# A recurrent scan of 128 steps: state and input stacked in one 128-row tile, one state and one output matmul a step, its input loaded from the loop's last iteration

## The chip, the core and the metric

The kernel runs on one core of a Trainium2 chip. The metric is the device time of one execution in microseconds (us). A core has TensorE (matmuls, fp32 here, in two passes each), VectorE, ScalarE, GpSimd and SyncE (SP), which issues the DMAs. Each works through its own instruction stream; they meet at semaphores.

## The reference, cut to what matters

The program is four attention blocks over 128 sequences of 128 positions and 256 features, and then a small recurrent layer, the scan. The change touches the scan:

```python
U = (xn @ W_in.T + b_in) @ Bmat            # 128 sequences x 128 positions x 64

def step(s, u_t):
    s = silu(s @ A.T) + u_t                # 64 states a sequence
    return (s, s)
_, states = lax.scan(step, zeros((128, 64)), U.transpose(1, 0, 2))
ssm_out = einsum('tbs,sh->bth', states, Cmat)   # 64 -> 256
x = residual + ssm_out
return x + mod[:, None, :]
```

All is fp32. The sequence of steps can't be parallelised: step n needs the state of step n-1, of all 128 sequences.

## The kernel before

There are four parts. A **prologue** loads weights (SP, lines 372 to 410) and prepares constants. The **loop** works on two sequences an iteration, in software pipelining: `drive` (line 235) issues, on each engine, a list of steps with a lag each; after the last full iteration come six partial ones, in which ever fewer steps are left. It leaves two tensors in HBM: `residual` (x before the scan, with mod added) and `u_turned` (U with the 64 states outermost, for each sequence 64 rows of 128 positions). SP's last steps in the loop are the stores of both. A **small block** (lines 1368 to 1384) clears tiles and loads the scan's constants and U. The **scan** (from line 1386) is the last block.

In the scan of before, half the sequences are on partitions 0 to 63 and half on 64 to 127. `u_all` (in the tile scan_u) holds U, `a2` is A.T twice on the diagonal of a 128x128 tile, and gbuf holds g = silu(...) of a step, without U, in four buffers of 64 columns. In step n:
- TensorE adds A u(n-1) (line 1460) and A g(n-1) (line 1463) in one bank, with 64 columns each;
- ScalarE applies silu to it into gbuf (line 1479);
- GpSimd adds g and u in two instructions of 64 partitions into the tile `sblk`, one for each half of the sequences (line 1437), since the output needs the sequences beside each other;
- TensorE makes the output of step n-1, with sblk as the stationary operand and C of 64 rows used twice as the moving one (line 1450, 256 columns), in one of two banks;
- VectorE adds it to the residual in SBUF (line 1488).

The elements of u_all that one step reads are 128 positions, 512 bytes, apart. The residual comes in 16 chunks of 8 positions, 1 MB each, in four buffers (SP: `load`, line 1402, and `store`, line 1406). On the four engines the first 32 steps are written out and the other 96 are a loop of three turns of 32 steps (`chunks`), with addresses and semaphore values from registers there.

Of the kernel before, what the change touches and what calls it, by code (L numbers as in the profile page):

```python
# [19 lines left out]
ALU = mybir.AluOpType  # L20
# [4 lines left out]
G = 2  # L25
NG = B // G
# [208 lines left out]
def drive(eng, rings, handlers, engine):  # L235
# [15 lines left out]
    for i in range(max(NG, LAGS + 1), NG + LAGS):  # L251
        body(i, LAGS + 2 + i - NG, False)


def build(nc, dram):
# [6 lines left out]
    with ExitStack() as ctx:  # L262
# [3 lines left out]
        def sem(name):  # L266
# [10 lines left out]
        wt = {n: sb("w_" + n, [128, DH, D]) for n in  # L277
              ("q1", "k1", "v1", "q2", "k2", "v2", "fc1", "fc2", "q3", "k3", "v3", "o3")}
# [13 lines left out]
               ("X", "XR", "CB", "Z1", "X1", "X1r", "Z2", "X2", "X3", "CC", "HC", "NF", "CR", "NC", "X4", "X5",  # L292
                "H5", "ATT", "X6", "H6")}
        trn_all = sb("turned", [128, 19, DH, W])
# [3 lines left out]
        scan_u = sb("scan_u", [128, B // 2 * S])  # L298
        keys12 = scan_u[:, 0:4 * DH * W].rearrange("p (k a h w) -> p k a h w", k=2, a=DH, h=2)
        keys1, keys2 = keys12[:, 0, :, :, :], keys12[:, 1, :, :, :]  # L300
        keys3 = sb("keys3", [128, DH, W])
        half_of = sb("half_of", [128, 2])
        vp1 = sb("vp1", [128, G, L0_HEADS, 32])
        vp2 = sb("vp2", [128, G, L0_HEADS, 32])
        vp3 = sb("vp3", [128, G, L3_HEADS, 64])
        vn1 = sb("vn1", [128, G, D])
        vn2 = sb("vn2", [128, G, D])
# [52 lines left out]
        ctxb_sb = scan_u[:, 0:S // 2 * NP].rearrange("p (s n) -> p s n", n=NP)  # L360
# [9 lines left out]
        with nc.Block() as block:  # L370
            @block.sync
            def _(sp):
                n = 0
                for name, t in wt.items():
# [38 lines left out]
        with nc.Block() as block:  # L413

            @block.vector
            def _(dve):
# [3 lines left out]
                nc.vector.memset(ones_b[:], 1.0)  # L420
                nc.vector.memset(half[:], -0.5)
# [75 lines left out]

        with nc.Block() as block:
            @block.sync
            def _(sp):  # L500
# [29 lines left out]

                def store_u(g):
# [4 lines left out]
                drive(sp, [], dict(self_in=dict(load=load_self), self_att=dict(load=load_again), ctx_in=dict(load=load_ctx),  # L536
                                   pair=dict(load=load_pair), mix_out=dict(load=load_mod, store=store, store_u=store_u)), "sp")
                for w in latest(res_out.done(NG - 1), u_out.done(NG - 1)):
                    sp.wait_ge(*w)

# [718 lines left out]
            def _(pool):  # L1259
# [74 lines left out]
                def mod_(g):  # L1334
# [13 lines left out]

        HB = B // 2
        NB = 4
        CHUNKS = S // TC
        u_all = scan_u[:].rearrange("p (b t) -> p b t", t=S)
        a2 = nat["X"][:, 0, 0:128]
        c2 = nat["CB"][:, 0, :]
        gbuf = [nat["Z1"][:, n // 2, (n % 2) * HB:(n % 2) * HB + HB] for n in range(4)]
        sblk = [nat["Z2"][:, n, 0:128] for n in range(2)]
        res_t = [trn_all[:, 4 * n:4 * n + 4, :, :].rearrange("p k a w -> p (k a w)").rearrange("p (t d) -> p t d", d=D)
                 for n in range(NB)]  # L1360
        vbank, obank = pbank[0:2], pbank[2:4]

        started, scan_in, v_ready, g_ready, s_ready, o_ready, out_ready = (
            sem(n) for n in ("started", "scan_in", "v_ready", "g_ready", "s_ready", "o_ready", "out_ready"))
        res_in = [sem(f"res_in{n}") for n in range(NB)]
        chunk_out = [sem(f"chunk_out{n}") for n in range(NB)]

        with nc.Block() as block:
            @block.vector
            def _(dve):  # L1370
                nc.vector.memset(nat["X"][:], 0.0)
                nc.vector.memset(nat["Z1"][:], 0.0)
                nc.vector.memset(nat["Z2"][:], 0.0).then_inc(started, 1)
                dve.wait_ge(started, 1)

            @block.sync
# [182 lines left out]
```

## Time and profile before

| | us |
|---|---|
| median of 3 runs | 4868.46 (4865.99 to 4876.72) |
| profiled execution | 4871.74, its span 4869.9 |
| loop with its ends, to the last store of u | up to 4678.9 |
| small block, until the scan opens | 4708.23 |
| scan | 4708.2 to 4869.9 |

The page gives TensorE 95% busy over the span, VectorE 76%, ScalarE 57%, GpSimd 45%. These shares are those of the loop. The mean granted TensorE clock is 0.975 of full; it is 0.5 while TensorE idles between loop and scan. In a timeline row the first two numbers are start and duration in us; what stands in brackets is the idle time of the engine before it and who ended it. PEld is the load of the stationary operand, PE the passes of the moving one; "x2" merges the two passes of an fp32 matmul. SPq is the issue of a DMA.

### The profile page before, as it was taken

Reading aid. Unit: us, or ns where it says so; the run is one execution under the profiler, and the core shown is the slowest. Engines: PE = TensorE matmul, PEld = TensorE weight load, DVE = VectorE, ACT = ScalarE, POOL = GpSimd, SP = SyncE. Lnnn points to the kernel's source line nnn. Section 1 sums busy time; section 2 is a strip of 40 time slices with the busy share of each in tenths; the row PEclk is TensorE's granted clock in tenths of the full one; section 3 lists DMA queues with packets and bytes.
Section 4 is the critical chain, followed back from the end, with each engine's and each line's share of the span. In section 5 each row is a group of like instructions: output and inputs, shape, how many; then the busy total and the mean of one; then the engine's idle time right before and its main releaser. Section 6 shows DMA issues by size and latency. Waiting matters only on the chain. (4 is left out here: it accounts for less than half of the span.)

```text
span 4869.9 us, 129469 instructions
## 1 busy us (share of the span) xinstructions
PE 4604.4 (95%) x38435; PEld 3800.8 (78%) x38563; DVE 3718.0 (76%) x10020; ACT 2760.2 (57%) x5761; POOL 2179.1 (45%) x2308
## 2 busy tenths in 40 slices
PE   2899999999999999999999999999999999999858
PEld 1678888888888888888888888888888888887647
DVE  2677888788878887887788888878888888788623
ACT  0456665666566656655665666556656665666411
POOL 0344444444444445444544454444444444444325
PEclk9899999999999999999999999999999999999879
DMA  3000000000000000000000000000000000000045
GB/s 92 18 19 22 26 22 28 21 24 25 28 21 22 26 28 21 21 27 28 21 21 27 28 21 21 27 28 21 21 27 28 21 21 27 27 21 20 20 122 199
DMA packets 139569, 156.21 MB, mean 32 GB/s; under 512 B 23942, under 2 KB 126667, under 8 KB 134859
## 3 DMA queue, kind: packets, MB, share of 16 engines
q1 hardware_dynamic: 139210, 152.93, 10.2%
q14 instruction: 316, 2.58, 0.2%
q8 instruction: 43, 0.70, 0.1%
HBM read 115.01 MB, written 37.88 MB: 31 GB/s over the span
## 5 line engine op out<-in xcount | busy, mean ns | idle before, releaser
L868 ACT ACTIVATE probT<-bank 128x512 f32<-128x512 f32 x1280 | 713.0, 594 | 604.9 <-PE bank L612 597.1
L1002 DVE TENSOR_REDUCE mx<-bank 128x4 f32<-128x512 f32 x1280 | 848.6, 680 | 200.2 <-PE bank L593 131.9
L1013 DVE TENSOR_TENSOR prob<-bank,mx 128x512 f32<-128x512 f32 x1280 | 870.9, 685 | 158.4 <-PE bank L612 137.4
L858 ACT ACTIVATE prob<-prob 128x512 f32<-128x512 f32 x1280 | 785.1, 629 | 189.1 <-DVE prob L1013 188.2
L848 ACT ACTIVATE turned<-bank 128x512 f32<-128x512 f32 x960 | 561.2, 601 | 438.2 <-PE bank L548 331.2
L1266 POOL TENSOR_TENSOR rs_ln<-ve_ln,half 128x2 f32<-128x2 f32 x320 | 226.1, 706 | 1182.5 <-DVE ve_ln L981 1182.5
L612 PE MATMUL bank<-ident,prob 128*128 128x128 f32 x5120 | 700.1, 278 | 43.1 <-ACT outT L878 41.3
L612 PEld LDWEIGHTS bank<-ident,prob 128*128 128x128 f32 x5120 | 587.6, 145 | 111.0 <-ACT prob L858 61.5
L597 PE MATMUL bank<-scan_u,turned 32*128 32x256 f32 x4096 | 493.7, 404 | 4.0 <-DVE X L1186 3.0
L1313 POOL TENSOR_SCALAR scan_u<-turned,half_of 128x512 f32<-128x512 f32 x256 | 399.4, 1571 | 118.7 <-ACT turned L848 118.7
L597 PEld LDWEIGHTS bank<-scan_u,turned 32*128 32x128 f32 x4096 | 321.1, 186 | 163.1 <-issue 142.4
L1275 POOL TENSOR_TENSOR X<-X,row_ln_g 128x512 f32<-128x512 f32 x192 | 244.3, 1273 | 446.9 <-DVE X L990 446.9
L556 PE MATMUL bank<-turned,w_q 128*128 128x256 f32 x1536 | 373.0, 386 | 1.4 <-ACT turned L848 1.4
L556 PE MATMUL bank<-turned,w_k 128*128 128x256 f32 x1536 | 372.1, 385 | 0.0
L564 PE MATMUL bank<-w_v,turned 128*128 128x256 f32 x1536 | 359.1, 383 | 0.5 <-ACT probT L868 0.3
L564 PEld LDWEIGHTS bank<-w_v,turned 128*128 128x128 f32 x1536 | 287.5, 190 | 41.3 <-ACT probT L868 0.4
L556 PEld LDWEIGHTS bank<-turned,w_k 128*128 128x128 f32 x1536 | 283.8, 191 | 39.0 <-issue 1.3
L556 PEld LDWEIGHTS bank<-turned,w_q 128*128 128x128 f32 x1536 | 279.9, 192 | 33.0 <-ACT turned L848 2.2
L642 PE MATMUL bank<-probT,vp 128*32 128x128 f32 x8192 | 293.2, 278 | 1.6 <-DVE vp L1100 1.0
L878 ACT ACTIVATE outT<-bank 128x512 f32<-128x512 f32 x384 | 221.7, 595 | 112.4 <-PE bank L642 90.5
L642 PEld LDWEIGHTS bank<-probT,vp 128*32 128x32 f32 x8192 | 201.8, 110 | 91.4 <-issue 64.8
L655 PE MATMUL bank<-ident,outT 128*128 128x128 f32 x1536 | 248.5, 286 | 3.2 <-ACT outT L878 3.2
(210 smaller groups left out, 8886.5 us busy)
## 6 DMA issues: line engine op xcount, KB each, us to landing
X<-in_x SPq DMA_DIRECT2D x64, 256.0 KB, 2.8
XR<-in_x SPq DMA_DIRECT2D x64, 256.0 KB, 2.7
CB<-in_ctx SPq DMA_DIRECT2D x64, 256.0 KB, 2.9
CC<-in_ctx SPq DMA_DIRECT2D x64, 256.0 KB, 2.7
mod<-mod_rows SPq DMA_DIRECT2D x64, 256.0 KB, 3.8
residual<-X SPq DMA_DIRECT2D x64, 256.0 KB, 2.2
turned<-residual SPq DMA_DIRECT2D x16, 1024.0 KB, 6.8
out<-turned SPq DMA_DIRECT2D x16, 1024.0 KB, 4.8
```

The lines of the kernel that those rows point to most:

```text
L556: last = nc.tensor.matmul(t[:, m * W:(m + 1) * W], w[:, a, m * 128:(m + 1) * 128], src[:, a, :], start=(a == 0), stop=(a == DH - 1))
L564: last = nc.tensor.matmul(t[:, b * D:(b + 1) * D], src[:, a, b * S:(b + 1) * S], w[:, a, :], start=(a == 0), stop=(a == DH - 1))
L597: last = nc.tensor.matmul(t[:, a * W:(a + 1) * W], QT[p][rows_, a, b * S:(b + 1) * S], KEYS[p][rows_, a, :, b * S:(b + 1) * S], start=(p ! ...
L612: last = nc.tensor.transpose(t[:, h * 128:(h + 1) * 128], src[:, h, :], ident[:])
L642: last = nc.tensor.matmul(t[k * 32:(k + 1) * 32, r * 128:(r + 1) * 128], VP[p][:, b, 4 * r + k, :], src[:, k, :], start=True, stop=True)
L655: last = nc.tensor.transpose(t[:, c * 128:(c + 1) * 128], outsT.of(key)[:, c, :], ident[:])
L848: nc.scalar.activation(dst, banks.of(f"{unit}.{name}")[:, 0:n], ACT.Copy).then_inc(*st["act"].mark(name))
L858: nc.scalar.activation(flat(t), flat(t), ACT.Exp, scale=SCALE[p]).then_inc(*st["act"].mark(f"exp.{b}{r}"))
L868: nc.scalar.activation(flat(t), banks.of(f"{att}.turn.{b}{r}")[:, :], ACT.Copy).then_inc(*st["act"].mark(f"probT.{b}{r}"))
L1002: nc.vector.tensor_reduce(m[:], banks.of(f"{att}.tile.{b}{r}")[:, :].rearrange("p (h t) -> p h t", h=4), AX, ALU.max)\
L1013: nc.vector.tensor_tensor(t[:], banks.of(f"{att}.tile.{b}{r}")[:, :].rearrange("p (h t) -> p h t", h=4), maxes.of(f"{att}.max.{b}{r}")[:]. ...
L1313: last = nc.gpsimd.tensor_scalar(KEYS[p][:, :, c, :], KT[p][:], half_of[:, c:c + 1], None, ALU.mult)
```

## The change

**One tile.** `shared`, 128 partitions x 16384, takes what scan_u held, and during the loop also eight weight tiles, the two x tiles and others. In the scan its partitions 64 to 127 hold U for all 128 sequences (`fresh`), and partitions 0 to 63 hold g of all steps (`state`), which ScalarE writes. So column t of sequence b has g above and u below. `a_two` is A.T twice, one below the other (columns 64 to 127 are zero), `c_two` is C twice. One matmul with 128 rows then sums both parts: A g + A u for the state, C g + C u for the output. There is no sum on GpSimd, and the output has four banks. TensorE's 128 steps are written out now; ScalarE, VectorE and SP keep their loops.

**The load.** `drive` takes a function `meanwhile` that is called at the start of the last partial iteration, only on SP: `scan_early` waits for the last readers of what it overwrites and loads U and four residual chunks of 126 sequences. The last two sequences' part comes behind the loop. The small block is gone; a_t and c_mat are loaded at the start of the prologue.

```diff
-def drive(eng, rings, handlers, engine):
+def drive(eng, rings, handlers, engine, meanwhile=None):
     for i in range(max(NG, LAGS + 1), NG + LAGS):
+        if meanwhile is not None and i == NG + LAGS - 1:
+            meanwhile()
         body(i, LAGS + 2 + i - NG, False)
...
+        shared = sb("shared", [128, B * S])
+        wt = {n: lent(DH, D) for n in ("q1", "k1", "v1", "q2", "k2", "v2", "fc1", "fc2")}
+        x_own, x_again, vn1, vn2 = (lent(G, D) for _ in range(4))
+        a_two = sb("a_two", [128, 128])
+        c_two = sb("c_two", [128, D])
-        scan_u = sb("scan_u", [128, B // 2 * S])
...
+                for k in range(2):
+                    r = slice(NS * k, NS * k + NS)
+                    sp.dma_start(a_two[r, 0:NS], dram["a_t"]).then_inc(loaded, 16)
+                    sp.dma_start(c_two[r, :], dram["c_mat"]).then_inc(loaded, 16)
...
+        EARLY = B - G
+        gu = shared[:].rearrange("p (b t) -> p b t", t=S)
+        state, fresh = gu[0:NS, :, :], gu[NS:2 * NS, :, :]
+        vbank, obank = pbank[0:2], pbank[2:6]
+        def scan_input(sp, b):
+            sp.dma_start(fresh[:, b, :], u_d[b].rearrange("b n s -> n b s")).then_inc(u_in, 16)
+            for k in range(NB):
+                sp.dma_start(res_t[k][b, :, :], res_d[b, k * TC:(k + 1) * TC, :]).then_inc(res_in[k], 16)
...
+                def scan_early():
+                    n = NG - 1
+                    for w in latest(self_in["pe"].done("xT", n), ..., u_out.done(n - 1), res_out.done(n - 1)):
+                        sp.wait_ge(*w)
+                    scan_input(sp, slice(0, EARLY))
...
                 for w in latest(res_out.done(NG - 1), u_out.done(NG - 1)):
                     sp.wait_ge(*w)
+                scan_input(sp, slice(EARLY, B))
...
-        with nc.Block() as block:     # memsets; loads of a_t, c_mat and u, 64 partitions each
...
-            @block.gpsimd             # s = g + u, two tensor_tensor a step
...
-                    nc.tensor.matmul(obank[k][:, 0:D], sblk[k], c2, start=True, stop=True).then_inc(o_ready, 1)
-                        nc.tensor.matmul(v[:, 0:HB], a2, u_all[:, :, bass.ds(n - 1, 1)], start=True, stop=False)
-                        nc.tensor.matmul(v[:, 0:HB], a2, gbuf[(t - 1) % 4], start=False, stop=True).then_inc(v_ready, 1)
+                def output(n):
+                    if n >= 4:
+                        pe.wait_ge(out_ready, n - 3)
+                    nc.tensor.matmul(obank[n % 4][:, 0:D], gu[:, :, n], c_two[:], start=True, stop=True).then_inc(o_ready, 1)
+                pe.wait_ge(u_in, 32)
+                pe.wait_ge(zeroed, 1)
+                for n in range(1, S):
+                    if n >= 2:
+                        pe.wait_ge(g_ready, n - 1)
+                    nc.tensor.matmul(vbank[n % 2][:, 0:B], a_two[:], gu[:, :, n - 1], start=True, stop=True).then_inc(v_ready, 1)
+                    output(n - 1)
...
-                        nc.scalar.activation(gbuf[t % 4], vbank[t % 2][:, 0:HB], ACT.Silu).then_inc(g_ready, 1)
+                        nc.scalar.activation(state[:, :, bass.ds(n, 1)], vbank[t % 2][0:NS, 0:B].unsqueeze(2), ACT.Silu).then_inc(g_ready, 1)
...
+                nc.vector.memset(state[:, :, 0:1], 0.0).then_inc(zeroed, 1)
```

The order of SP's instructions at the end of the loop, before the change (residual and u_turned are the tensors in HBM, started is the semaphore of the memsets):

```order
L529 DMA residual<-X 128x2x256 [waits mix_out_pool_6]
L534 DMA u_turned<-us 64x2x128 [waits mix_out_dve_6]
L498 UNCONDITIONAL_BRANCH [waits u_out,res_out]
L1376 UNCONDITIONAL_BRANCH [waits barrier_Pool_Activation_PE_DVE_SP_release]
L1381 DMA X<-in_a_t 64x64 [waits started]
L1382 DMA CB<-in_c_mat 64x256
L1383 DMA scan_u<-u_turned 64x64x128
L1381 DMA X<-in_a_t 64x64
L1382 DMA CB<-in_c_mat 64x256
L1383 DMA scan_u<-u_turned 64x64x128
L1368 UNCONDITIONAL_BRANCH [waits scan_in]
```

And the same place after it:

```order
L567 DMA residual<-X 128x2x256 [waits mix_out_pool_6]
L532 DMA shared<-u_turned 64x126x128 [waits ffn_pe_3,ctx_att_pe_3,pair_pe_4,ctx_att_pe_2,real_pe_4,ctx_in_dve_3,mix_in_pe_4,self_att_pe_1,mix_in_pe_5,self_att_dve_2,u_out,self_in_pool_1,res_out,self_in_dve_2,self_in_pe_0]
L534 DMA turned<-residual 126x2048 x4
L584 DMA u_turned<-us 64x2x128 [waits mix_out_dve_6]
L532 DMA shared<-u_turned 64x2x128 [waits u_out,res_out]
L534 DMA turned<-residual 2x2048 x4
L536 UNCONDITIONAL_BRANCH
```

The last store of residual stays first; the large loads of the scan stand between it and the last store of u_turned.

On ScalarE, the loop of the scan before the change (one step is two rows; v_ready is counted up by the state matmul):

```order
L1478 REGISTER_ALU [waits s_ready]
L1479 ACTIVATE Z1<-bank0 128x64 [waits v_ready]
L1478 REGISTER_ALU [waits s_ready]
L1479 ACTIVATE Z1<-bank1 128x64 [waits v_ready]
L1391 REGISTER_ALU
```

And after it:

```order
L1459 REGISTER_ALU
L1460 ISA [waits v_ready]
L1460 ACTIVATE shared<-bank1 64x128
L1459 REGISTER_ALU
L1460 ISA [waits v_ready]
L1460 ACTIVATE shared<-bank0 64x128
```

The wait for the matmul stood on the ACTIVATE, and stands now on the instruction ahead of it, which works out the destination's address.

## Rows read from the trace of the kernel before

**Rows 1.** Who waited for whom, from 4650 us: total us, times, longest us
```profile
ACT Z L1479 <- PE bank L1463: 125.4, 126, 2.2
DVE turned L1488 <- PE bank L1450: 98.5, 126, 1.1
```

**Rows 2.** Timeline of one step of the scan: start us, duration us, engine
```profile
4783.86 0.30 PEld L1463 LDWEIGHTS bank<-Z,X 128*128 128x128 f32 x2
4783.95 0.35 PE L1463 MATMUL bank<-Z,X 128*128 128x64 f32 x2
...
4784.34 0.22 ACT L1479 ACTIVATE Z<-bank 128x64 f32<-128x64 f32 x1 [0.86 <-PE bank L1463]
...
4784.55 0.70 PE L1450 MATMUL bank<-CB,Z 128*128 128x256 f32 x2 [0.25 <-POOL Z L1437]
4784.78 0.78 POOL L1437 TENSOR_TENSOR Z<-Z,scan_u 64x64 f32<-64x64 f32 x2 [0.29 <-issue]
```

**Rows 3.** Timeline: the first and the last of the scan's 127 ACTIVATEs
```profile
4709.52 0.23 ACT L1479 ACTIVATE Z<-bank 128x64 f32<-128x64 f32 x1
...
4863.15 0.22 ACT L1479 ACTIVATE Z<-bank 128x64 f32<-128x64 f32 x1 [0.77 <-PE bank L1463]
```

**Rows 4.** Lines 1460 and 1450, 4709.6 to 4711.5: ns min/median/max (clock 0.5)
```profile
L1460 PE MATMUL bank<-scan_u,X x2: 314/360/407, 4710.1 to 4710.2; 128*128 128x64 f32 x2
L1450 PE MATMUL bank<-CB,Z x4: 634/688/741, 4709.1 to 4711.4; 128*128 128x256 f32 x4
```

**Rows 5.** Lines 1450, 1463, 1460, 4716 to 4865: ns min/median/max (clock 1.0)
```profile
L1450 PE MATMUL bank<-CB,Z x248: 379/407/483, 4716.1 to 4864.7; 128*128 128x256 f32 x124
L1463 PE MATMUL bank<-Z,X x244: 235/264/275, 4716.8 to 4862.8; 128*128 128x64 f32 x122
L1460 PE MATMUL bank<-scan_u,X x244: 269/287/354, 4716.6 to 4862.7; 128*128 x96, 128*128 128x64 f32 x26
L1460 PEldq FUSED_REGOPS  x96: 37/37/51, 4747.2 to 4862.0; - x96
```

**Rows 6.** VectorE groups in the prologue: shapes, busy us, mean ns, idle
```profile
L447 DVE TENSOR_REDUCE X<-scan_u 128x64 f32<-128x4096 f32 x2 | 14.0, 6978 | 7.5 <-DMA scan_u<-in_ctxb 7.5
...
L428 DVE MEMSET vp<- 128x16 f32 x1 | 0.1, 72 | 0.0
L426 DVE MEMSET y<- 128x10 f32 x1 | 0.1, 67 | 0.0
```

**Rows 7.** Timeline at the loop's end: weights that wait for an ACTIVATE
```profile
4665.31 0.60 ACT L848 ACTIVATE turned<-bank 128x512 f32<-128x512 f32 x1 [2.92 <-PE bank L548]
4665.96 0.50 PEld L564 LDWEIGHTS bank<-w_o,turned 128*128 128x128 f32 x2 [1.15 <-ACT turned L848]
```

**Rows 8.** Timeline of SP's DMA issues between loop and scan
```profile
4675.73 0.38 SPq L529 DMA_DIRECT2D residual<-X  x1
4678.89 0.60 SPq L534 DMA_DIRECT2D u_turned<-us  x1
4683.22 0.54 SPq L1381 DMA_DIRECT2D X<-in_a_t  x1
4683.81 0.59 SPq L1382 DMA_DIRECT2D CB<-in_c_mat  x1
4684.45 0.63 SPq L1383 DMA_DIRECT2D scan_u<-u_turned  x1
4685.12 7.08 SPq L1381 DMA_DIRECT2D X<-in_a_t  x1
...
4692.88 0.62 SPq L1383 DMA_DIRECT2D scan_u<-u_turned  x1
4708.23 1.29 SPq L1402 DMA_DIRECT2D turned<-residual  x3
```

**Rows 9.** A stretch of three residual loads: last column GB/s
```profile
4712.00:4717.00 5.00, 3.35 (x23) 2.95 (x22) 1.78 (x5) 0.67 (x3) 2.35 (x7) 1.00 1.02 431
```

**Rows 10.** DMA issues, 4676 to 4712 us: count, KB each, median us to landing
```profile
u_turned<-us SPq DMA_DIRECT2D x1, 64.0 KB, 2.1
```

More of the change, by code:

```diff
@@ L420, in _ @@
                 nc.vector.memset(ones_b[:], 1.0)
+                nc.vector.memset(a_two[:, NS:128], 0.0)
                 nc.vector.memset(half[:], -0.5)
@@ L536, in _ @@
                 drive(sp, [], dict(self_in=dict(load=load_self), self_att=dict(load=load_again), ctx_in=dict(load=load_ctx),
[L537 removed]
+                                   pair=dict(load=load_pair), mix_out=dict(load=load_mod, store=store, store_u=store_u)), "sp", scan_early)
                 for w in latest(res_out.done(NG - 1), u_out.done(NG - 1)):
                     sp.wait_ge(*w)
+                scan_input(sp, slice(EARLY, B))
             @block.tensor
@@ L1346, in _ @@
                     real=dict(**ln_pow("ln5", "real")), mix_out=dict(**ln_pow("ln6", "mix_out"), mod=mod_)), "pool")
[L1351 to L1366, printed above, removed]
-        with nc.Block() as block:
[L1369 to L1376, printed above, removed]
-            def _(sp):
-                sp.wait_ge(started, 1)
-                for k in range(2):
-                    r = slice(NS * k, NS * k + NS)
-                    sp.dma_start(nat["X"][r, 0, NS * k:NS * k + NS], dram["a_t"]).then_inc(scan_in, 16)
-                    sp.dma_start(nat["CB"][r, 0, :], dram["c_mat"]).then_inc(scan_in, 16)
-                    sp.dma_start(u_all[r, :, :], u_d[k * HB:(k + 1) * HB].rearrange("b n s -> n b s")).then_inc(scan_in, 16)
-                sp.wait_ge(scan_in, 96)
         with nc.Block() as block:
@@ L1422, in _ @@
                     sp.wait_ge(chunk_out[k], 16 * (CHUNKS // NB))
-            @block.gpsimd
-            def _(pool):
-                def body(c, k, _):
-                    for t in range(TC):
-                        n = c * TC + t
-                        waits = []
-                        if at_least(n, 1):
-                            waits.append((g_ready, n))
-                        if at_least(n, 2):
-                            waits.append((o_ready, n - 1))
-                        waits_apart(pool, prep, *waits)
-                        for half_ in range(2):
-                            r = slice(NS * half_, NS * half_ + NS)
-                            last = nc.gpsimd.tensor_tensor(sblk[t % 2][r, half_ * HB:(half_ + 1) * HB], gbuf[t % 4][r, :],
-                                                           u_all[r, :, bass.ds(n, 1)].rearrange("p b t -> p (b t)"), ALU.add)
-                        last.then_inc(s_ready, 1)
-                chunks(pool, body)
@@ L1466, in _ @@
-                chunks(pe, body)
-                output(S - 1, (S - 1) % 2)
+                def output(n):
[9 more added lines that the diff above has]
+                    output(n - 1)
@@ L1469, in _ @@
+                pe.wait_ge(g_ready, S - 1)
+                output(S - 1)
             @block.scalar
```

65 lines of the change are left out of this document (32 added, 33 removed).

## The prediction

> **What bounds the kernel now.** I read the page's slices first: 39 of 40 show the pipelined loop, in which the change moves no instruction, and the last holds the scan over the 128 positions. So only three stretches can move: the prologue, the hand-over between loop and scan, and the scan. Next I read the waits from 4650 us on [rows 1]. In the scan ScalarE stands 125.4 us waiting for the state matmul, VectorE 98.5 us for the output matmul; nothing is busy all the time, so it is a cycle of dependences. One step of its timeline [rows 2] shows which one: the state pass ends (4783.95 + 0.35 = 4784.30), ScalarE starts at 4784.34 and ends at 4784.56, GpSimd starts the sum only at 4784.78, and TensorE starts an output at 4784.55 that had waited for the sum before. From the first ScalarE step (4709.52) to the last (4863.15) [rows 3] are 153.6 us for 126 steps, 1.22 us each. From the last to the end of the span are 6.7 us.
>
> **The step after the change.** GpSimd leaves the cycle, and TensorE issues two matmuls instead of three. The outputs have four banks, so VectorE's addition does not hold them. What is left is one chain: weights of the state matmul, its two passes (fp32 runs as two) of 128 columns, ScalarE, and back. TensorE's own work besides, the output, has two passes of 256 columns; it lies beside ScalarE.
>
> Cost of a column. At the granted clock of 0.5 (1.2 GHz) a pass of 256 columns takes 634 ns and one of 64 takes 314 [rows 4]: 320 ns for 192 columns, 1.67 ns each, so 0.83 ns at the full clock (2.4 GHz). At the full clock 256 columns take at least 379 ns [rows 5], which is 213 + 166 of pipeline. A pass of 64 neighbouring columns (line 1463) should be 53 + 166 = 219, and its shortest is 235. But line 1460, whose 64 columns lie 512 bytes apart in scan_u, takes at least 269: 269 - 166 = 103 ns, 1.61 ns a column, about twice. At the half clock the same line shows nothing of this (314 is from it). The new moving operand is always of this kind, 128 columns 512 bytes apart, so a pass costs 206 ns and not 107. VectorE pays alike: its sum over elements 256 bytes apart takes 6978 ns for 4096, 1.70 ns each [rows 6]. The Trainium skill (SBUF — State Buffer, section Door 1: The DMA port swizzle) says that SBUF has lines of 16 bytes and that each access that goes to a new line pays a penalty; by it the passes are slow as taken here, and without it a step would be two times 99 ns shorter. The trace agrees for reads.
>
> One step, while ScalarE's addresses are constants (steps 1 to 31): load of weights 108 ns (the two loads of line 1463 in rows 2 span 0.30 at 0.19 each, so the second starts about 0.11 behind the first), first pass 206, second pass 206 + 166, to ScalarE 40 (rows 2: 4784.30 to 4784.34), ScalarE 275, back to TensorE 50 (an ACTIVATE ends at 4665.91, the weights that wait for it load at 4665.96) [rows 7]. ScalarE's 275: 64 elements take 0.22 us and 512 take 0.60 [rows 2, 7], 0.85 ns each, so 64 more are 55. Sum 1.05 us. TensorE alone would need 2 x 206 + 2 x 213 = 0.84 us, with the weight loads beside the passes; even if the strided weights of the output load at half speed (206 ns, which the trace does not show) they lie beside passes of at least that length. So the chain decides.
>
> In the 96 steps of the loop there is something more. Today ScalarE's destination is one of four fixed buffers, and the wait for the matmul sits on the ACTIVATE itself. Now the destination is a column whose address comes from a register: the order shows an ISA row (the address calculation, which carries the wait) ahead of each ACTIVATE, so the ACTIVATE is only sent off when the matmul is done. Nearest rows: this calculation takes 37 to 51 ns on TensorE [rows 5], and GpSimd, which today does the same for scan_u, starts 0.22 us after the ScalarE step that it waits for [rows 2], against 0.05 where the wait sits on the instruction [rows 7]. So the price is between 0.04 and 0.17 us; I take 0.12, nearer to GpSimd since it is the same construction. Loop step: 1.17 us.
>
> Scan from first to last ScalarE step: 30 x 1.05 + 96 x 1.17 = 143.8, and 0.7 for some three steps at the half clock, since TensorE comes from idleness: 144.5 against 153.6. **Gain 9.1 us.** Behind the last step GpSimd's sum is gone and the load of strided weights comes, 5.9 against 6.7: **gain 0.8**.
>
> **The hand-over.** Today SP sends the last residual store at 4675.73, the last u at 4678.89, and after a barrier and three memsets the two halves of u at 4684.45 and 4692.88; the last block opens at 4708.23 [rows 8]. The new early load stands in SP's program behind the last residual store, and that waits for GpSimd's last instruction until 4675.7. So it is not sent an iteration earlier, but at 4675.73 + 0.38 and fifteen waits that are long fulfilled, about 4676.9: 7.5 us sooner than today. And it is larger: the input of 126 sequences and four residual chunks (4.1 MB of input, 4.1 MB of residual), and only then the store of the last u, on which the last two sequences' input depends. All are on one queue: in today's order the second a_t load, sent from 4685.1 to 4692.2 behind the first half of u, took 7.1 us to send. Input: today 23.8 us from the first issue to the opened block, of which I put 0.4 down to the barrier (an estimate, from 0.1 to 0.8), so landed at 4700.3. Residual: at 431 GB/s [rows 9] 9.6 us: 4709.9. Last u: 64 KB, 0.3 us; late input: 2.1 us from issue to landing, as the last u today [rows 10], and SP sends four more small loads (0.63 for the first, 1.29 for three of the others: 2.3 us) before it comes to the barrier: 4712.5. With barrier 0.3 the block opens at 4712.8, against 4708.23: **loss 4.5 us**. Today VectorE also waits for its first residual chunk when the scan opens; that stall is in the 153.6 already. Bounds: 3 (the barrier does not wait for the small loads) to 7. If the last u got in between, the start would be at some 4702, a gain of 6; the order of the queue speaks against it. The Trainium skill (DMA: Bandwidth & Descriptors, section Why a DMA increments its semaphore by 16 and not by 1) says that a DMA runs on the largest number of engines up to 16 that divides its slowest dimension; 126 rows would get 14, an estimate of 1.4 us more for the four residual loads, by which the loss would be 5.9. No run here shows it yet.
>
> **The prologue.** Four more loads stand first in SP's program; the same loads took 0.54 and 0.59 us to send today [rows 8], 2.4 with gaps. Part goes where SP stands at a full queue later: between 0 and 2.4, I take **loss 2**. The memset of a_two is 0.1 us, inside that.
>
> **Sum.** -9.1 - 0.8 + 4.5 + 2 = -3.4 us on the profiled execution's 4871.74 (its span is 4869.9). The median of the runs shown is 4868.46, 3.3 lower; I subtract the same amount: 4865.1 us. A change of 0.2% (9.7 us) is about what a measurement of this kernel can tell from none, so this is no change.
>
> **Rivals.** (1) The stride costs nothing (the ends of matmuls are modelled, so 269 might be a model's). Then the step is 0.198 us shorter, 126 x 0.198 = 25 us: 4840. Against it stand two engines that agree, and the half clock, where it vanishes. Chance 0.12. (2) The address calculation is hidden or costs its 0.04: 96 x 0.08 to 0.12, 8 to 11 us: 4856. For it: ScalarE has 0.77 us idle in each step; against it: the wait sits on it, so it cannot run ahead. Chance 0.20. (3) Slower: ScalarE's write pays for the stride too. It writes 128 elements, 512 bytes apart, and at 1.61 instead of 0.83 ns they take 100 ns more on the chain: 126 x 0.1 = 12.6 us, 4878. It turns slower than before as soon as a written element costs 0.21 ns more than today (3.4 us over 126 x 128 elements). Against it: a memset of 16 elements 256 bytes apart takes 72 ns, one of 10 neighbours 67 [rows 6], 0.8 ns for each of six more, so a short strided write pays nothing on VectorE. The skill's rule does not set writes apart, and by it this is the result. Chance 0.16. (4) The change does not load early in effect: the queue makes the start later still (7 us or more, 4868 and above). Chance 0.07. The forecast has the rest, 0.45.
>
> **How the numbers follow.** Forecast and (4) are within 0.2% nearly always; (1) is faster always, (2) about half the time, and in the forecast a smaller calculation with a smaller stride gives faster once in eight: 0.12 + 0.10 + 0.05, about 0.27. Slower needs (3) with little help from the hand-over, or two of the high bounds: 0.18. Same 0.55. The range leaves out most of (1) and takes in (3): 4846 to 4881.
>
> **What would show it.** In the new profile: the ACTIVATE of 128 elements lasts 275 ns (370 or more: rival 3); the state matmul's shortest first pass 206 + 166 = 372 ns (273: rival 1); the ScalarE steps lie 1.05 us apart in the first 31 and 1.17 in the loop (equal: rival 2); the first TensorE instruction of the scan stands between 4714 and 4716, 2 us of it from the prologue. The forecast is wrong if TensorE, or VectorE, is what ScalarE's successors wait for, or if the loop before the scan changes by more than 2 us.

## The result: 0.5% slower

| | before | after |
|---|---|---|
| median, us | 4868.66 (6 runs, 4862.24 to 4876.72) | 4893.49 (6 runs, 4890.14 to 4900.58) |
| span of the profiled execution | 4869.9 | 4894.6 |

The ratio is 1.0051, 95% interval 1.0039 to 1.0064. The forecast was 4865.1, its range ended at 4881. The two spans differ by 24.7 us, and ScalarE's instructions cut them into five stretches:

| stretch, us | before | after | difference | forecast |
|---|---|---|---|---|
| start to the first ScalarE step of all (prologue) | 96.54 | 99.83 | +3.3 | +2 |
| to the last ScalarE step of the loop | 4579.06 | 4582.91 | +3.9 | 0 |
| to the first ScalarE step of the scan (hand-over) | 33.92 | 42.99 | +9.1 | +4.5 |
| to the scan's last ScalarE step | 153.63 | 162.80 | +9.2 | -9.1 |
| to the end | 6.75 | 6.07 | -0.7 | -0.8 |

The other four stretches are 20.9 us, and they are to be explained. Of the second, 3.9 us, the cause is open. Over the twelve profiles of this case whose kernels have the changed kernel's loop it lies between 4575.0 and 4590.7 us, and of the loop of before there is one profile, so the two profiles alone can't tell. But the medians hint at a real part: for the changed kernel and each of the six experiments below that have several runs, the median differs from that of before by 0.7 to 9.9 us more than its other four stretches do (24.8 against 20.9 for the changed kernel). The prediction named a loop that changes by more than 2 us as a sign that it is wrong, and no experiment here tests why the loop would.

### The profile page after: what moved, and what is told of

The parts are those of the page before. It is cut to its first block and busy times, and to the rows that moved or that the text cites. A ratio compares the mean times of both kernels' runs of the same rounds, so it can differ in the third digit from the quotient of the medians.

```text
span 4894.6 us, 128116 instructions
## 1 busy us (share of the span) xinstructions
PE 4629.2 (95%) x38309; PEld 3801.4 (78%) x38309; DVE 3719.5 (76%) x10019; ACT 2777.4 (57%) x5761; POOL 2084.0 (43%) x2052
## 5 line engine op out<-in xcount | busy, mean ns | idle before, releaser
L607 PE MATMUL bank<-turned,shared 128*128 128x256 f32 x2560 | 616.1, 384 | 0.7 <-ACT turned L899 0.7
L607 PEld LDWEIGHTS bank<-turned,shared 128*128 128x128 f32 x2560 | 465.1, 192 | 56.6 <-ACT turned L899 1.3
L648 PE MATMUL bank<-shared,turned 32*128 32x256 f32 x4096 | 495.8, 406 | 4.0 <-DVE X L1237 3.0
L1364 POOL TENSOR_SCALAR shared<-turned,half_of 128x512 f32<-128x512 f32 x256 | 399.1, 1570 | 123.1 <-ACT turned L899 123.1
L648 PEld LDWEIGHTS bank<-shared,turned 32*128 32x128 f32 x4096 | 323.1, 187 | 163.1 <-issue 142.0
L615 PE MATMUL bank<-shared,turned 128*128 128x256 f32 x1536 | 359.8, 384 | 0.6 <-ACT probT L919 0.3
L615 PEld LDWEIGHTS bank<-shared,turned 128*128 128x128 f32 x1536 | 283.4, 191 | 38.4 <-DVE turned L1160 0.5
L693 PE MATMUL bank<-probT,shared 128*32 128x128 f32 x8192 | 292.8, 278 | 1.9 <-DVE shared L1151 1.0
L1332 POOL TENSOR_TENSOR X<-X,row_ln_b 128x512 f32<-128x512 f32 x192 | 243.7, 1269 | 15.1
L644 PE MATMUL bank<-keys,turned 32*128 32x128 f32 x2048 | 221.6, 286 | 3.8 <-DVE prob L1064 3.2
```

What stands on the lines that cost most here:

```text
L607: last = nc.tensor.matmul(t[:, m * W:(m + 1) * W], w[:, a, m * 128:(m + 1) * 128], src[:, a, :], start=(a == 0), stop=(a == DH - 1))
L615: last = nc.tensor.matmul(t[:, b * D:(b + 1) * D], src[:, a, b * S:(b + 1) * S], w[:, a, :], start=(a == 0), stop=(a == DH - 1))
L648: last = nc.tensor.matmul(t[:, a * W:(a + 1) * W], QT[p][rows_, a, b * S:(b + 1) * S], KEYS[p][rows_, a, :, b * S:(b + 1) * S], start=(p ! ...
L693: last = nc.tensor.matmul(t[k * 32:(k + 1) * 32, r * 128:(r + 1) * 128], VP[p][:, b, 4 * r + k, :], src[:, k, :], start=True, stop=True)
L1364: last = nc.gpsimd.tensor_scalar(KEYS[p][:, :, c, :], KT[p][:], half_of[:, c:c + 1], None, ALU.mult)
```

## The profile after

Waits from 4670 us (who waited for whom: total, times, longest), the answer to [rows 1]:

```profile
ACT shared L1460 <- PE bank L1447: 115.1, 126, 1.2
DVE turned L1471 <- PE bank L1440: 111.5, 128, 1.9
PEld bank L1447 <- ACT shared L1460: 51.6, 126, 0.7
...
PEld bank L1447 <- DMA shared<-u_turned: 40.3, 1, 40.3
```

The cycle is the expected one: ScalarE and TensorE wait for each other 126 times, and GpSimd is gone from it. VectorE waits for TensorE, and in the steps nobody waits for VectorE. The first and the last of the scan's ScalarE rows, and one step of the timeline among the first 31 (start, duration, engine; [rows 2, 3]):

```profile
4725.73 0.38 ACT L1460 ACTIVATE shared<-bank 64x128 f32<-64x128 f32 x1
...
4755.78 0.30 PEld L1447 LDWEIGHTS bank<-shared,a_two 128*128 128x128 f32 x2 [0.35 <-ACT shared L1460]
4755.78 0.75 PE L1447 MATMUL bank<-shared,a_two 128*128 128x128 f32 x2
...
4756.07 0.59 PEld L1440 LDWEIGHTS bank<-c_two,shared 128*128 128x128 f32 x2
4756.35 0.62 PE L1440 MATMUL bank<-c_two,shared 128*128 128x256 f32 x2
4756.57 0.38 ACT L1460 ACTIVATE shared<-bank 64x128 f32<-64x128 f32 x1 [0.84 <-PE bank L1447]
4757.00 0.30 PEld L1447 LDWEIGHTS bank<-shared,a_two 128*128 128x128 f32 x2 [0.34 <-ACT shared L1460]
...
4888.53 0.38 ACT L1460 ACTIVATE shared<-bank 64x128 f32 x1 [0.93 <-PE bank L1447]
```

A step lasts 4757.00 - 4755.78 = 1.22 us, and the load of the output's weights (4756.07 to 4756.66) lies beside the state matmul's second pass (to 4756.53). The durations by line, 4730 to 4888 us (ns min/median/max), answer to [rows 5]:

```profile
L1447 PEld LDWEIGHTS bank<-shared,a_two x246: 185/188/191, 4730.1 to 4887.8; 128*128 128x128 f32 x123
L1447 PE MATMUL bank<-shared,a_two x246: 464/468/472, 4730.1 to 4887.9; 128*128 128x128 f32 x123
...
L1460 ACT ACTIVATE shared<-bank x123: 377/378/381, 4729.6 to 4887.2; 64x128 f32 x95, 64x128 f32<-64x128 f32 x28
L1460 ACTq FUSED_REGOPS  x95: 37/37/37, 4763.9 to 4887.1; - x95
...
L1440 PE MATMUL bank<-c_two,shared x245: 376/379/409, 4729.6 to 4887.2; 128*128 128x256 f32 x123
L1440 PEld LDWEIGHTS bank<-c_two,shared x245: 302/359/366, 4730.4 to 4887.9; 128*128 128x128 f32 x123
```

Written as the forecast wrote it, in us:

| part of a step | forecast | measured |
|---|---|---|
| first load of weights | 0.108 | 0.107 |
| first pass, until the second starts | 0.206 | 0.184 |
| second pass | 0.372 | 0.468 |
| to ScalarE | 0.040 | 0.037 |
| ScalarE | 0.275 | 0.378 |
| back to TensorE | 0.050 | 0.050 |
| sum (first 31 steps) | 1.05 | 1.224 |
| address calculation, loop steps | 0.12 | 0.087 |
| loop step | 1.17 | 1.311 |

The hand-over, in the timeline of SP's issues, the answer to [rows 8]:

```profile
4682.87 0.38 SPq L567 DMA_DIRECT2D residual<-X  x1
4683.76 0.64 SPq L532 DMA_DIRECT2D shared<-u_turned  x1
4684.44 20.62 SPq L534 DMA_DIRECT2D turned<-residual  x4
4705.11 0.61 SPq L584 DMA_DIRECT2D u_turned<-us  x1
4721.88 0.63 SPq L532 DMA_DIRECT2D shared<-u_turned  x1
4722.55 1.34 SPq L534 DMA_DIRECT2D turned<-residual  x4
```

The DMA issues of this stretch (count, KB each, median us to landing) and two windows of it (last columns granted clock, DMA share, GB/s; [rows 9, 10]):

```profile
shared<-u_turned SPq DMA_DIRECT2D x1, 4032.0 KB, 25.9
...
u_turned<-us SPq DMA_DIRECT2D x1, 64.0 KB, 16.7
shared<-u_turned SPq DMA_DIRECT2D x1, 64.0 KB, 2.4
```
```profile
4688.00:4703.00 15.00, 0.00 (x0) 0.00 (x0) 0.00 (x0) 0.00 (x0) 0.00 (x0) 0.50 1.25 176
4706.00:4718.00 12.00, 0.00 (x0) 0.00 (x0) 0.00 (x0) 0.00 (x0) 0.00 (x0) 0.50 0.97 306
```

The store of the last u is sent at 4705.11 and lands 16.7 us later, since the residual is ahead of it on the queue. The last two sequences' input leaves only at 4721.88 and lands 2.4 us later, at 4724.23. Behind it SP sends the four small residual loads before it comes to the barrier, and VectorE clears the first state only behind that:

```profile
4724.56 0.17 DVE L1466 MEMSET shared<- 64x128 f32 x1 [38.56 <-PEq L536]
4724.84 0.29 PEld L1447 LDWEIGHTS bank<-shared,a_two 128*128 128x128 f32 x1 [40.25 <-DMA shared<-u_turned]
```

So TensorE starts at 4724.84. Its row names the input, but that had landed 0.6 us earlier: the barrier and the memset are what ends last.

## Experiments: where the step's time goes

Two steps are given for each kernel: one of the first 31 (ScalarE's addresses constant) and one of the loop. The changed kernel has 1.224 and 1.311.

**Neighbouring columns (e1).** The same tile, viewed with the sequences as neighbours:

```diff
+        gt = shared[:].rearrange("p (t b) -> p t b", b=B)
-  output: gu[:, :, n]          state: gu[:, :, n - 1]     silu: state[:, :, bass.ds(n, 1)]
+  output: gt[:, n, :]          state: gt[:, n - 1, :]     silu: gt[0:NS, bass.ds(n, 1), :]
```

> The changed kernel, but in the scan the tile is read and written as (position, sequence): the 128 elements of a step lie beside each other, for ScalarE's write, for the moving operand of the state matmul and for the stationary one of the output. U is loaded as before, so the numbers pair wrong positions and sequences; the amount of work is the same. Theory S (every access 512 bytes apart costs extra on the chain): ACTIVATE 378 -> 275 ns; state passes from 468 and 468 ns to about 380 (the first, which waits for its weights) and 273; loads of the output's weights 359 -> 190; step 1.22 -> 0.85 us in the 31 written-out steps and 1.31 -> 0.94 in the loop, first to last ACTIVATE 162.8 -> 116 us, span about 4848. Rival X (the chain is long because of 128 columns on 64 partitions and of two matmuls with weights to load, wherever they lie): nothing of this falls by more than 20 ns, span about 4894.

The step behaves as theory S says, in each of its parts, and nothing stays as rival X would have it. Measured: 4854.6 us (one run), steps 0.848 and 0.945, 116.8 us from first to last ACTIVATE. One step of its timeline:

```profile
4749.83 0.30 PEld L1448 LDWEIGHTS bank<-shared,a_two 128*128 128x128 f32 x2 [0.33 <-ACT shared L1461]
4749.84 0.49 PE L1448 MATMUL bank<-shared,a_two 128*128 128x128 f32 x2
...
4750.05 0.30 PEld L1441 LDWEIGHTS bank<-c_two,shared 128*128 128x128 f32 x2
...
4750.36 0.27 ACT L1461 ACTIVATE shared<-bank 64x128 f32<-64x128 f32 x1 [0.58 <-PE bank L1448]
4750.68 0.30 PEld L1448 LDWEIGHTS bank<-shared,a_two 128*128 128x128 f32 x2 [0.33 <-ACT shared L1461]
```

With the same instructions the pair of passes is 0.49 instead of 0.75, ScalarE 0.27 instead of 0.38, the output's weights (two loads) 0.30 instead of 0.59. So the distance of 512 bytes between elements costs 0.376 us of a step of 1.224, 46 us of the scan.

VectorE's write doesn't pay it. In the changed kernel it clears a column of 128 elements 512 bytes apart, in e1 128 neighbours, and both take 165 ns (groups of VectorE, mean ns behind the busy us; the changed kernel first):

```profile
L1466 DVE MEMSET shared<- 64x128 f32 x1 | 0.2, 165 | 38.6 <-PEq L536 38.6
```
```profile
L1467 DVE MEMSET shared<- 64x128 f32 x1 | 0.2, 165 | 38.9 <-PEq L537 38.9
```

**Only the write beside (e2), only the weights beside (e3), both (e10).** ScalarE writes into another tile whose columns are neighbours, or the output reads its weights from one, or both; the state matmul reads as before.

```diff
-  silu: state[:, :, bass.ds(n, 1)]     zeros: state[:, :, 0:1]      # e2, e10
+  silu: keys3[0:NS] as rows, columns bass.ds(n, 128)     zeros: state[:, :, :]
-  output: gu[:, :, n]                                               # e3, e10
+  output: nat["Z1"][:, 0, 0:128]
```

> The changed kernel, but ScalarE writes its 128 elements beside each other in another tile (keys3), at an address from a register as before; the state rows of the tile are cleared once when the scan opens (14 us that only move its start) and stay zero, so the recurrence is left out. All reads stay 512 bytes apart. Theory S: ACTIVATE 378 -> 275 ns, step 1.22 -> 1.12 and 1.31 -> 1.21 us, state passes stay at 468 ns, first to last ACTIVATE 162.8 -> 150. Rival W (378 ns comes from the form, 128 elements read from PSUM on 64 partitions): ACTIVATE stays at 378, and 162.8 stays.

> The changed kernel, but the stationary operand of the output matmul is a fixed tile of 128 neighbouring columns, so the output leaves the state out; everything else is as in the changed kernel, the state matmul's moving operand and ScalarE's write 512 bytes apart. Theory C (two reads of TensorE at 512 bytes, the output's weights and the second state pass, slow each other): the loads fall from 359 to 190 ns and the second state pass from 468 to about 370 ns, step 1.22 -> 1.13 and 1.31 -> 1.22 us, first to last ACTIVATE 162.8 -> 151. Rival L (a pass of 128 columns at this distance simply takes 300 ns): only the loads fall, the pass stays at 468, and 162.8 stays.

> The changed kernel with both e2's and e3's edits: ScalarE writes beside, the output's weights are a fixed tile; only the moving operand of the state matmul still reads 512 bytes apart (recurrence and state are left out of the result). If the prices add up: 1.224 - 0.107 - 0.071 = 1.05 us a written-out step and 1.31 - 0.107 - 0.072 = 1.13 in the loop, first to last ACTIVATE about 141 us, and each of the two state passes takes some 80 to 100 ns more than with neighbours (e1's step was 0.85). If the second state pass still takes 390 ns or more, more than the weights slows it.

| | step | loop step | ACTIVATE, ns | output's LDWEIGHTS, ns | second state pass, ns |
|---|---|---|---|---|---|
| changed kernel | 1.224 | 1.311 | 378 | 302 to 366 | 468 |
| e2 | 1.117 | 1.204 | 272 | 302 to 370 | 468 |
| e3 | 1.154 | 1.239 | 380 | 206 | 396 |
| e10 | 1.045 | 1.131 | 271 | 206 | 395 |
| e1 | 0.848 | 0.945 | 272 | 192 | 275 |

Two rows of the view by line show the reading of e3 and e10, that of e3 first; the passes of a matmul have one line, and their median (431, 414) lies between a first pass of some 465 and a second of some 395:

```profile
L1447 PE MATMUL bank<-shared,a_two x166: 395/431/469, 4730.1 to 4829.8; 128*128 128x128 f32 x166
...
L1440 PEld LDWEIGHTS bank<-c_two,Z x165: 206/206/208, 4730.4 to 4829.8; 128*128 128x128 f32 x165
```
```profile
L1447 PE MATMUL bank<-shared,a_two x166: 393/414/550, 4739.0 to 4829.9; 128*128 128x128 f32 x166
...
L1460 ACT ACTIVATE keys<-bank x82: 270/271/273, 4739.8 to 4829.3; 64x128 f32 x51, 64x128 f32<-64x128 f32 x31
```

The prices add up: the write costs 0.107, the output's weights 0.071 (they slow the state's second pass beside them), and e10 is 0.179 below the changed kernel, the sum of both. The moving operand itself is the rest to e1, 0.197, the 2 x 99 ns of the forecast. It stands 77 ns on the first pass (0.184 against 0.107 until the second starts) and 120 on the second (395 against 275). The expectation of e10 took a second pass of 390 ns or more as a sign that more than the weights slows it. It is 395, but the first pass is short by as much, and the two together, 0.579, are the 0.578 that the forecast has for strided passes alone: no further slowing is needed. E3's weights gave 0.071 where up to 0.098 was expected: the second pass gets 72 ns shorter, and the sum of load and passes, 0.107 + 0.184 + 0.396 = 0.687, is then the forecast's 0.686. The memset of e2 and e10, over the whole state, starts their scans 17 to 19 us later, so their times (4904.56 and 4887.77) say nothing of the step.

**ScalarE's steps written out (e4).**

```diff
-                chunks(act, body)
+                for c in range(CHUNKS):
+                    body(c, c % NB, 0)
```

> The changed kernel with ScalarE's 127 steps written out, so that every address is a constant and the wait sits on the ACTIVATE. Theory A (the address calculation that carries the wait costs 0.087 us in each of 96 steps): all steps 1.22 us, first to last ACTIVATE 162.8 -> 154.5, time 8.4 us less (4885). Rival: the loop's steps are longer because of TensorE or of contention with the transfers: they stay at 1.31 and the time within 3 us.

Measured: steps 1.224 and 1.226, 154.85 us, as expected; so the address from a register costs 0.087 us a step, 8 us in all. The median is 4887.07 (7 runs), ratio 1.0033 (1.0021 to 1.0044), 6.4 lower than the changed kernel's. In the profiled execution the hand-over gave 5.0 back: its residual packets of 8 KB took 401 ns (median) where the changed kernel's took about 320.

## Experiments: the hand-over and the prologue

**Residual behind the scan's opening (e5).** The four chunks leave `scan_input` and are loaded by SP's part of the scan.

```diff
             sp.dma_start(fresh[:, b, :], u_d[b].rearrange("b n s -> n b s")).then_inc(u_in, 16)
-            for k in range(NB):
-                sp.dma_start(res_t[k][b, :, :], res_d[b, k * TC:(k + 1) * TC, :]).then_inc(res_in[k], 16)
...
+                for k in range(NB):
+                    load(k, k)
```

> The changed kernel, but the early load is only the input; the four residual chunks are loaded by SP when the scan opens, whole, as before the change. Theory Q (one queue: the last u, which the late input needs, stands behind 4.1 MB of residual, 12 us): from the last residual store to the first ACTIVATE 42.9 -> about 31 us, then VectorE waits some 5 us for its first chunk and TensorE with its four banks waits a little, 1 us; time 11 us less (4882). Rival (the start hangs on the input's own 23 us or on the barrier): under 3 us less.

**The early load ahead of the last residual store (e6).** `scan_early` is called in the step `store` of the last iteration, before its DMA.

```diff
+                    if isinstance(g, int) and g == NG - 1:
+                        scan_early()
-  ... "sp", scan_early)
+  ... "sp")
```

> The changed kernel, but the early load (input and residual) stands ahead of the last residual store in SP's program, which waits 20 us for GpSimd's last instruction; the operands that it overwrites have been read by then. Theory P (the early load was late because of its place): its first issue comes at about 4665 instead of 4683.8 in the trace of the changed kernel, input landed at 4689, residual at 4702; the last u goes at 4702, the late input at 4704, first ACTIVATE about 17 us earlier; time 16 us less (4877). Rival (a wait of the early load itself, for the last readers, holds it till 4680): under 4 us less. Rival 2 (the transfers slow the loop's last iteration): the last residual store comes later than 20 us behind the one before.

Both hand-overs came as expected (e5's time 3 us longer than expected, e6's as expected). From the loop's last ScalarE step to the scan's first: 30.65 us in e5 and 24.41 in e6, against 42.99. Times: e5 4885.09 (7 runs), ratio 1.0027 (1.0015 to 1.0038); e6 4876.6 (9 runs), ratio 1.0018 (1.0007 to 1.0028). SP's issues in e6:

```profile
4660.77 0.64 SPq L532 DMA_DIRECT2D shared<-u_turned  x1
4661.46 20.33 SPq L534 DMA_DIRECT2D turned<-residual  x4
4681.83 0.44 SPq L569 DMA_DIRECT2D residual<-X  x1
4682.32 0.71 SPq L586 DMA_DIRECT2D u_turned<-us  x1
4699.02 0.64 SPq L532 DMA_DIRECT2D shared<-u_turned  x1
```

The load now leaves 17.7 us before the loop's last ScalarE step (4678.47), and the loop is not held up. The scan still waits for the late input, sent at 4699.02, and for what follows it, since the residual (until 4697.6) and the last u's store are ahead of it. So the order of the queue, and nothing that TensorE or ScalarE does, sets when the scan starts.

**Small loads out of the prologue (e8).** a_t and c_mat are loaded at the start of `scan_early`.

```diff
-  prologue, first DMAs: a_two and c_two, twice
+  scan_early, ahead of scan_input: a_two and c_two, twice
```

> The changed kernel, but a_t and c_mat are loaded at the head of the early load instead of at the head of the prologue. Theory P2 (four more sends of 0.6 us delay everything behind them): the first ACTIVATE of the program comes 3.3 us earlier (99.8 -> 96.5), the early load 2.4 us later; time 1 us less, within noise. Rival: the 3.3 us are from elsewhere (where the tiles lie): the first ACTIVATE stays at 99.8.

Measured: the first ScalarE step of all is at 96.42, so the four small loads do cost the prologue 3.4 us. But the hand-over is 47.88, 4.9 longer: 2.4 are the four issues, and the residual's packets took 375 ns in this execution, some 2 us more in all. The median is 4897.24 (4 runs), ratio 1.0058 (1.0041 to 1.0074), 3.7 over the changed kernel's where 1 less was expected; the ranges of their runs overlap. The 3.4 us are not seen in the time.

**112 sequences early instead of 126 (e9).** The late part has 16, the early input two transfers (64 and 48 sequences).

```diff
-        EARLY = B - G
+        EARLY = B - 16
...
-                    scan_input(sp, slice(0, EARLY))
+                    sp.dma_start(fresh[:, 0:64, :], u_d[0:64].rearrange("b n s -> n b s")).then_inc(u_in, 16)
+                    sp.dma_start(fresh[:, 64:EARLY, :], u_d[64:EARLY].rearrange("b n s -> n b s")).then_inc(u_in, 16)
...
```

> The changed kernel, but the early load takes 112 sequences instead of 126, and its input goes in two transfers, of 64 and 48 sequences; 16 sequences come late. Theory K (126 rows run on 14 of 16 engines, as the largest divisor up to 16): 112 rows run on 16, a residual chunk takes 7 packets an engine of 0.31 us, 2.2 instead of 3.0 us, all four 8.7 instead of 12.0. Rival: bandwidth of HBM, 112/126 of 12.0, 10.7 us. For the input: packets of 512 bytes came at 400 per us before the change, in transfers of 64 sequences, and at 343 in one of 126. If the size of the transfer does it, 400 per us again; if it is the place in the tile, 343 again.

Measured: 4902.48 us (one run), hand-over 45.33. Its issues, of 4680 to 4740:

```profile
turned<-residual SPq DMA_DIRECT2D x4, 896.0 KB, 17.1
shared<-u_turned SPq DMA_DIRECT2D x1, 2048.0 KB, 14.8
shared<-u_turned SPq DMA_DIRECT2D x1, 1536.0 KB, 23.2
shared<-u_turned SPq DMA_DIRECT2D x1, 512.0 KB, 6.4
```

The early input still moves 338 packets a us (changed kernel: 341; before: 385), so splitting it changes nothing. The Trainium skill (DMA: Bandwidth & Descriptors, section Why a DMA increments its semaphore by 16 and not by 1) gives a transfer of 126 rows 14 engines and one of 112 rows 16. The trace agrees with the counts: the durations of the residual's packets add up to about 14 at a time in the changed kernel and to about 16 here. But here each took 466 ns (median) against 322, and 448 packets took 14.4 us from the first start to the last where 504 took 13.2; theory K expected 8.7, its rival 10.7. More engines brought no more bytes. That the count explains the slow residual is not borne out, in this one run; why its packets take 309 to 466 ns (medians) from one execution to another is open.

## Experiments: a version that beats both kernels

**A ring (e7).** Eight places of 128 neighbouring columns (halves of the tiles Z1 and Z2) hold one step each. ScalarE writes g into the upper half, GpSimd copies the step's U into the lower one, ahead of time, and both matmuls read neighbours. ScalarE is written out, the input leaves ahead of the last residual store (as e6), the residual behind the opening (as e5), the small loads behind the prologue (as e8, ahead of the early load).

```diff
+        ring = [nat[z][:, a, 128 * h:128 * h + 128] for z in ("Z1", "Z2") for a in range(2) for h in range(2)]
+                    pe.wait_ge(p_ready, n)
                     if n >= 2:
                         pe.wait_ge(g_ready, n - 1)
-  state matmul: gu[:, :, n - 1]        silu: state[:, :, bass.ds(n, 1)]
+  state matmul: ring[(n - 1) % 8]      silu: ring[n % 8][0:NS, :]
+            @block.gpsimd
+                    if n >= 8:
+                        pool.wait_ge(o_ready, n - 7)
+                    nc.gpsimd.tensor_copy(ring[n % 8][NS:2 * NS, :], fresh[:, :, n]).then_inc(p_ready, 1)
```

> A version built from what the runs showed. (1) The 128 rows of a step stand in a ring of eight small tiles with the sequences beside each other: GpSimd, which has nothing to do in the scan, copies U of a step into rows 64 to 127 ahead of time, ScalarE writes g into rows 0 to 63; all addresses are constants, ScalarE and GpSimd are written out. (2) The early input load stands ahead of the last residual store, the residual chunks are loaded when the scan opens, a_t and c_mat with the early load. By the runs before: step 0.85 us in all 127 steps, first to last ACTIVATE 107 to 112 us (low clock at first, and a wait for the first residual chunk), from the last ACTIVATE of the loop to the first of the scan some 12 us, prologue as before the change: 4801 us, 68 under the kernel before. Rival G: GpSimd's copy of 128 elements 512 bytes apart takes over 0.8 us with its wait and becomes the bound: first to last over 115 us, ScalarE's predecessor waits for GpSimd: 4810 or more.

Measured: 4816.71 us (5 runs), ratio 0.9893 (0.9877 to 0.9910); hand-over 15.33, steps 0.913 throughout, 115.8 us. It was expected at 4801 and 0.85. The numbers are those of rival G, in which GpSimd's copy is the bound (4810 or more, over 115 us), and the step is 0.065 over e1's. A wait row and GpSimd in the timeline:

```profile
PEld bank L1451 <- POOL Z L1463: 46.8, 120, 0.4
```
```profile
4760.13 0.30 PEld L1451 LDWEIGHTS bank<-Z,a_two 128*128 128x128 f32 x2 [0.39 <-POOL Z L1463]
...
4760.21 0.40 POOL L1463 COPY Z<-shared 64x128 f32<-64x128 f32 x1 [0.51 <-PE bank L1443]
...
4760.66 0.27 ACT L1473 ACTIVATE Z<-bank 64x128 f32<-64x128 f32 x1 [0.64 <-PE bank L1451]
4761.04 0.30 PEld L1451 LDWEIGHTS bank<-Z,a_two 128*128 128x128 f32 x2 [0.39 <-POOL Z L1463]
```

The row blames GpSimd, as rival G would, and it is wrong: its copy takes 0.40 us and is done at 4760.61, 0.43 before the weights load at 4761.04, and it is of a place used six steps later. ScalarE ends at 4760.93, and the load comes 0.11 later, not 0.05. The state matmul has two waits, and the trace has an instruction of its own for the one on ScalarE, 51 ns on TensorE, ahead of the load.

**One wait on the state matmul (e11).**

```diff
-                    pe.wait_ge(p_ready, n)
                     if n >= 2:
                         pe.wait_ge(g_ready, n - 1)
                     nc.tensor.matmul(vbank[n % 2][:, 0:B], a_two[:], ring[(n - 1) % 8], start=True, stop=True).then_inc(v_ready, 1)
+                    pe.wait_ge(p_ready, n + 1)
                     output(n - 1)
```

> As the ring kernel (neighbouring columns, GpSimd lays U of each step beside the place where ScalarE writes, small loads behind the loop, input sent before the last residual store, residual behind the scan's opening). The only edit: TensorE waits for GpSimd's copy of step n+1 ahead of the output of step n-1 and no longer ahead of the state matmul, which keeps one wait, that for ScalarE. Theory W (the second wait on the state matmul is an instruction of its own on the chain, and is what the ring's step of 0.913 us has over the 0.848 us of the kernel with neighbouring columns alone): the step falls by 0.05 to 0.065 us to 0.85 to 0.86, from first to last ACTIVATE about 108 us instead of 115.8, and the time by 7 us to about 4809. Rival V (the step is longer because of what the ring itself does: ScalarE writing 128 columns from a row of another tile, or GpSimd's copies beside it): the step stays at 0.91, the time at 4816. Rival T (the wait moved ahead of the output makes the output late enough for TensorE to hold the next state matmul): the step is above 0.91.

```profile
PEld bank L1451 <- ACT Z L1473: 40.8, 126, 0.3
```
```profile
4760.37 0.27 ACT L1473 ACTIVATE Z<-bank 64x128 f32<-64x128 f32 x1 [0.58 <-PE bank L1451]
4760.69 0.30 PEld L1451 LDWEIGHTS bank<-Z,a_two 128*128 128x128 f32 x2 [0.33 <-ACT Z L1473]
```

Measured: steps 0.849, 108.3 us from first to last ACTIVATE, and the wait is named rightly now. The time is 4811.83 us (4 runs), ratio 0.9886 (0.9869 to 0.9902): 1.1% faster than the kernel before. That it is 4.9 below the ring is of the expected size, but the two intervals overlap; it is the step, 0.064 shorter, that shows theory W. Of the 93.6 us between its span (4801.0) and the changed kernel's, the scan has 54.5, the hand-over 27.8, the prologue 3.1 and the loop's variation 8.

## Why the prediction was wrong

- **"ScalarE 275": wrong, 378.** This is rival 3, which was given 0.16 and priced at 100 ns; e2 measures 107. It was put low on one row, the memset of 16 elements against 10 neighbours [rows 6]. The row was read rightly, and for VectorE it holds at full length too: a memset of 128 elements takes 165 ns at either distance (e1). What failed is the step from VectorE to ScalarE. The rows that spoke for rival 3 (two engines pay on reads) were taken not to bear on writes. Cost: 126 x 0.103 = 13 us.
- **"Second pass 206 + 166": wrong, 468.** The forecast saw the strided weights of the output lie beside the state's pass and asked only whether they would be late. They were not; but they slow the pass beside them, 396 to 468 (e3). Cost 126 x 0.071 = 9 us, for which no rival stood. The other 24 ns (372 to 396) only stand in another place: the first pass was 184 for 206. Forecast 1.051 + 0.103 + 0.071 = 1.225 against 1.224 measured. These two terms, 22 us, less 3 for the next one, turned the -9.1 into +9.2.
- **Address calculation 0.12: nearly right,** 0.087 (e4), 3 us in its favour. Rival 2 needed it hidden or at 0.04: false.
- **Stride on reads: right.** A moving operand 512 bytes apart costs 0.197 a step (e10 to e1), the 2 x 99 ns of the forecast, though 77 and 120 of it stand on the two passes; rival 1 is false. The Trainium skill (SBUF — State Buffer, section Door 1: The DMA port swizzle) makes no exception for writes, and the prediction did not follow it there. The trace agrees with the page for ScalarE's write, where the prediction did not, and not for VectorE's memset, where 165 ns are measured at both distances.
- **Hand-over +4.5: mis-sized, +9.1.** The early load was indeed sent only behind the last residual store (1.0 us behind ScalarE's last step, forecast 1.3), and the queue did put the last u behind the residual. From there: the input needed 25.2 us until its last packet ended, not 23.4 (it came at 176 GB/s); the residual 12.2, not 9.6 (306 GB/s, not the 431 of [rows 9]); from there to TensorE's first load of weights 3.7, not 2.9. That is 4.9 too little, 0.4 of it given back until the first ScalarE step. Of the residual's 2.6 us the forecast could have seen more than half: 431 GB/s is a stretch of 5 us in the middle of the loads of before, and the three of them as a whole moved 384 packets of 8 KB in 8.5 us, 370 GB/s, by which 4.1 MB take 11.2 us. The rest is open, as are the input's 1.8. Rival 4 (7 us or more) had a chance of 0.07 and came true.
- **Prologue +2: 3.3.** Its bound of 2.4 counted the time to send four loads. E8 shows the whole effect, 3.4.
- **Tail -0.8: right,** -0.7.

The rivals were priced one at a time. Rivals 3 and 4 came together, 12.6 + 4.9 on top of 4865.1 make 4882.6, above the range, which ended just above where rival 3 alone did. The slowed pass (9 us) and the open 3.9 of the loop did the rest. The forecast gain of 3.4 us was so small that rival 3, rival 4 or the slowed pass would each have turned its sign alone.

## What to carry to other kernels

When a tile is laid out so that a step reads or writes single fp32 elements far apart, price every access of it, writes and stationary operands too, by rows of the engine that makes it, and price what lies beside it as slowed, not as free. An early load is early only against what stands ahead of it on its queue; order the queue by who waits. On a chain, give the instruction that is waited for one wait, and a constant address.

## What the runs showed of the hardware

- 128 fp32 elements on a partition, 512 bytes apart against neighbours: ScalarE's write 378 against 272 ns, TensorE's weight load 302 to 366 against 192, its moving operand 197 ns more over the two passes at the full clock. VectorE's memset takes 165 ns in both. At a granted clock of 0.5 (1.2 GHz) the first pass of the state matmul takes 421 ns in both (the changed kernel at 4726.34, e1 at 4730.70). Strided weights beside a strided pass slow it from 396 to 468 ns (e3 against the changed kernel).
- A destination whose address is in a register costs 0.087 us on the chain, since the wait moves to the calculation (37 ns) ahead of the instruction. A second wait on a matmul costs 0.064 us (e7 to e11), and the profile named the wrong releaser there.
- Open: why the early input moves 341 packets of 512 bytes a us where the two loads of before moved 385; why packets of the same residual load take 309 to 466 ns (medians) in different executions; and whether the change lengthens the loop.
